# Attention and ternary feed-forward: transposes by halves of the tensor engine's rows, scores two steps behind the projection

## The reference

```python
# x = x + xattn(layernorm(x), ctx)
qh = einsum('bse,ehd->bshd', q, Wq)      # 16 heads of 32, in 4 groups
kh, vh = (einsum('bse,ehd->bshd', kv, W) for W in (Wk, Wv))   # 4 heads
qh, kh = rope(qh), rope(kh)
attn = softmax(einsum('bghsd,bhad->bhsa', qh, kh) / sqrt(32))  # sums over g
out = einsum('bhsa,bhad->bhsd', attn, vh).mean(axis=1) @ Wo
# x = x + ffn(layernorm(x)), weight ternary, input rounded to 8 bits by max|x|
out = einsum('bsk,ok->bso', clip(round(x / s), -128, 127), ternary(w)) * w_scale * s + bias
```

## Time and profile before

| | |
|---|---|
| Median of 3 runs | 1301.93 us |
| Profiled execution, its own time | 1300.03 us |
| Span of its instructions | 1298.1 us |
| Granted TensorE clock, mean | 0.993 |
| PE busy | 1265.4 us (97%), 9911 matmuls |
| Weight loads (PEld) | 1085.0 us (84%) |
| DVE busy | 1151.5 us (89%) |
| ACT busy | 1025.9 us (79%) |
| POOL busy | 792.1 us (61%) |
| Chain that ended last | PE 92%, DVE 4% |

### The profile page before, as it was taken

One profiled execution on the slowest core, in us unless ns is written; L12 is line 12 of the kernel. 1 busy time (PEld: TensorE's weight loads), 2 busy tenths in 40 slices (PEclk: granted clock), 3 DMA queues, 4 the chain that ended last, 5 costly groups with the idle time before them and its releaser, 6 DMA issues.

```text
span 1298.1 us, 36156 instructions
## 1 busy us (share of the span) xinstructions
PE 1265.4 (97%) x9911; PEld 1085.0 (84%) x9911; DVE 1151.5 (89%) x2577; ACT 1025.9 (79%) x2339; POOL 792.1 (61%) x1536
## 2 busy tenths in 40 slices
PE   7998999999999999999999999999969999999998
PEld 7898999999999999999999999999835555555554
DVE  4756999999999999999999999999978888888887
ACT  4565888888888888888888888888857888788876
POOL 4566888888888888888888888888810000000000
PEclk9999999999999999999999999999979999999999
DMA  9773455555555565546464633232109999999945
GB/s 297 225 207 105 140 177 166 170 171 167 175 161 181 152 189 151 190 144 196 143 197 141 197 116 103 75 105 73 37 32 362 405 397 397 405 396 405 398 202 223
DMA packets 101205, 265.26 MB, mean 204 GB/s; under 512 B 49833, under 2 KB 66153, under 8 KB 72498
## 3 DMA queue, kind: packets, MB, share of 16 engines
q1 hardware_dynamic: 101122, 264.79, 59.5%
q10 hardware_dynamic: 48, 0.07, 0.0%
HBM read 139.64 MB, written 125.17 MB: 204 GB/s over the span
## 4 chain that ended last, share of the span: by engine, by line
PE 92%; DVE 4%; issue 1%; POOL 1%; ACT 1%; DMA 0%; SPq 0%; POOLq 0%; DVEq 0%; ACTq 0%
PE bank L1156 17%; PE bank L1236 17%; PE bank L1204 13%; PE bank L1126 8%; PE bank L1191 8%; PE bank L1177 6%; PE bank L1227 4%; PE bank L1167 4%; PE bank L1234 4%; PE bank L1065 4%; PE bank L1138 2%; PE bank L1146 2%; PE bank L1054 1%; DVE amax L899 1%; DVE x_sb L929 0%
## 5 line engine op out<-in xcount | busy, mean ns | idle before, releaser
L1236 PE MATMUL bank<-wT,x_sb 128*128 128x512 f16 x1024 | 263.1, 379 | 0.0
L1156 PE MATMUL bank<-wqs,xT_sb 128*128 128x128 f32 x2048 | 259.7, 280 | 0.0
L731 ACT ACTIVATE x_sb<-bank,mean,cols 128x512 f32<-128x512 f32 x256 | 197.0, 775 | 66.6 <-PE bank L1236 66.5
L1156 PEld LDWEIGHTS bank<-wqs,xT_sb 128*128 128x128 f32 x2048 | 238.2, 191 | 6.6 <-ACT xT_sb L653 0.3
L1204 PE MATMUL bank<-v_blk,pT_sb 103*128 103x136 f32 x1536 | 199.0, 279 | 0.3 <-ACT pT_sb L695 0.3
L929 DVE SCALAR_TENSOR_TENSOR x_sb<-x_sb,mv_sb,bank 128x512 f32 (+1 forms) x256 | 179.9, 744 | 14.1 <-PE bank L1167 5.8
L1204 PEld LDWEIGHTS bank<-v_blk,pT_sb 103*128 103x128 f32 x1536 | 190.6, 190 | 0.5 <-ACT pT_sb L695 0.5
L1236 PEld LDWEIGHTS bank<-wT,x_sb 128*128 128x128 f16 x1024 | 100.4, 98 | 106.3 <-issue 0.8
L899 DVE TENSOR_REDUCE amax<-x_sb (+1 forms) x128 | 156.0, 1219 | 23.1 <-DVE bn_sb L890 10.1
L704 ACT ACTIVATE sq_sb<-x_sb 128x512 bf16 (+1 forms) x256 | 161.5, 631 | 18.7 <-DVE x_sb L929 1.4
L1004 DVE TENSOR_TENSOR x_sb<-x_sb 128x512 f32 (+1 forms) x256 | 164.7, 684 | 1.2 <-ACT x_sb L731 1.2
(11 more groups left out here) (132 smaller groups left out, 2558.2 us busy)
## 6 DMA issues: line engine op xcount, KB each, us to landing
out_y<-x_sb SPq DMA_DIRECT2D x112, 1024.0 KB, 7.2
x_sb<-in_x SPq DMA_DIRECT2D x64, 1024.0 KB, 6.4
x_sb<-out_y SPq DMA_DIRECT2D x48, 1024.0 KB, 8.9
x_sb<-in_ctx SPq DMA_DIRECT2D x38, 256.0 KB, 4.5
k_blk<-k_scr SPq DMA_DIRECT2D x256, 19.2 KB, 5.5
k_scr<-x_sb SPq DMA_DIRECT2D x38, 128.0 KB, 3.7
v_scr<-x_sb SPq DMA_DIRECT2D x38, 68.0 KB, 3.6
v_blk<-v_scr SPq DMA_DIRECT2D x128, 10.2 KB
```

What stands on the lines that cost most here:

```text
L731: act.activation(u_sb[:, t, :], bank[4 + t][:, :], ACT.Identity, bias=stat_of(mean1, j, t, back), scale=cols[:, 6:7]).then_inc(scaled_t, 1)
L1156: last = pe.matmul(bank[2][:, t * HD:(t + 1) * HD], xT_sb[:, t, c, :], wqs[:, c, :], start=c == 0, stop=c == EC - 1)
L1236: last = pe.matmul(bank[4 + t][:, :], q16T_sb[:, t, c, :], wT[:, c, :], start=False, stop=c == EC - 1)
```

## The change

In the main loop, every transpose of the tensor engine is written as two: rows 0 to 63 of the source and rows 64 to 127, into two neighbouring banks. The scores are plain float32, heads 0 and 1 on rows 0 to 63 and heads 2 and 3 on rows 64 to 127, into two banks; q and k are no longer split. PE's step begins with all transposes and the scores. A stage ROPE stands between PROJ and SCORE, so scores and all that follows are one step later. The orders of ACT, DVE and POOL within a step are changed. x is loaded by halves of a batch. On PE four of the waits take their value from registers. The keys' scratch and block have one part. Cut to its core:

```diff
-PROJ, SCORE, VALUE, HEAD, RESID, STAT, RSTD = range(7)
+HALF = P // 2
+PROJ, ROPE, SCORE, VALUE, HEAD, RESID, STAT, RSTD = range(8)
+xT_ps, qo_ps, sc_ps, pT_ps = (... psum_tensor(n, [P, 2, 512], F32) ...)
+bank = [ps[:, n, :] for ps in (xT_ps, qo_ps, sc_ps, pT_ps) for n in range(2)]
+def rows_of(ps, at0, n):
+    return ps[:, :, at0:at0 + n * HALF].rearrange("p h (c r) -> p c h r", c=n)
+def scores_of(t):
+    return sc_ps[:, :, t * SC // 2:(t + 1) * SC // 2].rearrange("p n (h a) -> p n h a", a=CTX)
 # SP
-sp.dma_start(x_sb[:, b, :, :], xv[b]).then_inc(x_in[b], 16)
+for n in range(2):      # in the loop each after at_least(sp, added_t, 4 * (b - XS) + 2 * n + 2)
+    sp.dma_start(x_sb[:, b, 2 * n:2 * n + 2, :], xv[b, :, 2 * n:2 * n + 2, :]).then_inc(x_in[2 * b + n], 16)
-                    batch_step(g * XS + k, k, g)
-                    kv_step(g * XS + k, k)
+                    batch_step(g * XS + k, k, g)
+                    v_fetch(g * XS + k - 1, k - 1)
+                    k_fetch(g * XS + k, k)
 # PE, one step
+def halves(ps, at0, src):
+    for n in range(2):
+        lo, hi = n * HALF, (n + 1) * HALF
+        last = pe.transpose(ps[0:src.shape[1], n, at0:at0 + HALF], src[lo:hi, :], ident[lo:hi, lo:hi])
+    return last
+if score or resid: at_least(pe, q_copied, i)
+if score:   # held: qr_ready
+    for t in range(2): last = halves(qo_ps, t * HALF, qr_sb[:, kj % 2, t * HD:(t + 1) * HD])
+if resid:   # held: ost_ready
+    for t in range(2): last = halves(qo_ps, P + t * HALF, ost_sb[:, t, ...])
+if proj:    # x_in, held: added_t >= 2 * (j - RESID)
+    for t in range(2):
+        for c in range(EC): last = halves(xT_ps, (t * EC + c) * HALF, x_sb[...])
+if value:   # pv_copied, held: exp_done_t
+    for t in range(2):
+        for c, start in enumerate(STARTS):
+            last = halves(pT_ps, (t * CHUNKS + c) * HALF, e_sb[:, kj % 2, t, start:start + CR])
+if score:   # k_in, sub_done_t >= 2 * j, qT_copied
+    for t in range(2):
+        for n in range(2):
+            lo, hi, w = n * HALF, (n + 1) * HALF, SC // 2
+            last = pe.matmul(sc_ps[:, n, t * w:(t + 1) * w], qT_sb[lo:hi, t * P:(t + 1) * P],
+                             k_blk[lo:hi, slot, n * w:(n + 1) * w], start=True, stop=True)
 # then, as before: projection (after oT_copied, xT_copied_t), y, values (after pT_copied_t)
 # ACT, one step:  pv, qT, oT, xT x2, pT x2, square(0), q, exponentials x2, square(1)
+act.activation(xT_sb[:, t, :, :].rearrange("p c (h r) -> p c h r", h=2),
+               rows_of(xT_ps, t * E // 2, EC), ACT.Copy).then_inc(xT_copied_t, 1)
 # DVE, one step:  reciprocal, variance (L876), amax, statistics 0, maxima x2, subtractions x2,
 #                 statistics 1, wait for them, residual adds x2, aggregates x2, wait, ve (L919)
-dve.tensor_tensor(qT_sb[:, 1, :], bank[3][:, 0:2 * P], qT_sb[:, 0, :].bitcast(F32), ALU.subtract)...
-    low_keys(j - 2)                       # setup: kT's low half, 39 times
 # POOL, one step: rope of pair i-1 (3), pw, pw2, rs, o, ost x2, mean, rs2
```

More of the change, by code:

```diff
@@ L518, in step @@
             def step(i, k, g):
[L519 to L525, removed]
+                proj, rope, score, value, head, resid, stat, rstd = (stage(i, k, g, lag) for lag in range(RSTD + 1))
+                if rope:
+                    j, kj, gj = rope
+                    at_least(pool, qr_ready, j)
+                    pool.wait_ge(q_copied, j + 1)
+                    half = slice(2 * (kj % 2), 2 * (kj % 2) + 2)
+                    for table, dst in ((qcos, qa_sb), (qsin, qb_sb)):
+                        pool.tensor_tensor(dst[:, :].rearrange("p (t h d) -> p t h d", t=2, h=HEADS),
+                                           q_sb[:, :].rearrange("p (t h d) -> p t h d", t=2, h=HEADS),
+                                           table[:, half, :].unsqueeze(2).broadcast_to([P, 2, HEADS, D]),
+                                           ALU.mult).then_inc(rope_mul, 1)
+                    at_least(pool, qT_done, j - 1)
+                    pool.wait_ge(rope_mul, 2 * j + 2)
+                    pool.tensor_tensor(qr_sb[:, kj % 2, :].rearrange("p (a b) -> p a b", b=2),
+                                       qa_sb[:, :].rearrange("p (a b) -> p a b", b=2),
+                                       swapped(qb_sb[:, :]), ALU.add).then_inc(qr_ready, 1)
                 if head:
@@ L560, in step @@
                                        ALU.add).then_inc(mean_ready, 1)
[L561 to L575, removed]
-                                       swapped(qb_sb[:, :]), ALU.add).then_inc(qr_ready, 1)
+                if rstd:
+                    j, kj, gj = rstd
+                    pool.wait_ge(var_ready, j + 1)
+                    pool.tensor_tensor(rs2[:, bass.ds(2 * j, 2)], ve2_sb[:, kj % 2, :], mhalf[:, :], ALU.pow)\
+                        .then_inc(rs2_ready, 1)
             steps(pool, step)
@@ L636, in step, with square @@
             def step(i, k, g):
-                proj, score, value, head, resid, stat, rstd = (stage(i, k, g, lag) for lag in range(RSTD + 1))
+                proj, rope, score, value, head, resid, stat, rstd = (stage(i, k, g, lag) for lag in range(RSTD + 1))
+                def square(t):
+                    j, kj, gj = stat
+                    act.wait_ge(added_t, 2 * j + t + 1)
+                    at_least(act, sq_done, 2 * j + t)
+                    act.activation(sq_sb[:, :], x1_at(kj, gj, t), ACT.Square,
+                                   accum_out=ssq[:, bass.ds(2 * j + t, 1)]).then_inc(sq_done, 1)
                 if head:
@@ L645, in step @@
                                    bank[6][:, 0:2 * HEADS * VC], ACT.Copy).then_inc(pv_copied, 1)
-                if proj:
-                    j, kj, gj = proj
-                    for t in range(2):
-                        act.wait_ge(xT_done_t, 2 * j + t + 1)
-                        if t == 0:
-                            at_least(act, q_done, j)
-                        act.activation(xT_sb[:, t, :, :].rearrange("p c r -> p (c r)"), bank[t][:, :],
-                                       ACT.Copy).then_inc(xT_copied_t, 1)
-                    if isinstance(j, int) and j == 0:
-                        keys_out(CT, CLAST)
                 if score:
@@ L1132, in step @@
+            def step(i, k, g):
+                proj, rope, score, value, head, resid, stat, rstd = (stage(i, k, g, lag) for lag in range(RSTD + 1))
+                if score or resid:
+                    at_least(pe, q_copied, min(i, NP_) if isinstance(i, int) else i)
                 if score:
                     j, kj, gj = score
-                    pe.wait_ge(qr_ready, j + 1)
+                    held(qr_ready, j + 1, qr_count, 1)
                     for t in range(2):
-                        last = pe.transpose(bank[3][:, t * P:(t + 1) * P], qa_sb[:, t * HD:(t + 1) * HD],
-                                            ident[:, :])
+                        last = halves(qo_ps, t * HALF, qr_sb[:, kj % 2, t * HD:(t + 1) * HD])
```

282 lines of the change are left out of this document (136 added, 146 removed).

## The result

| | before | after |
|---|---|---|
| Median | 1303.12 us (4 runs) | 1268.89 us (4 runs, 1268.15 to 1269.79) |
| Ratio to before, 95% interval | | 0.9739 (0.9722 to 0.9756) |
| Profiled execution | 1300.03 us | 1268.90 us |
| PE / DVE / ACT / POOL busy | 97 / 89 / 79 / 61% | 95 / 89 / 79 / 63% |

The change gains 2.6%. I had forecast 1263 us.

What follows compares the result with a forecast made beforehand. PE bounds the kernel at 6.552 us a pair; relieved to 5.98, it yields to DVE at 6.18, rounded to 6.20. 123 periods give -43.3, ends +4.1: 1260.8, plus 1.9 for the median, 1263 us; range 1236 to 1296.

Steps and rivals of the forecast that it cites:

- the forecast's own range: Whole kernel's time: 1250 to 1277 us around the forecast of 1263, given a chance of 0.54.
- Transposes by halves: PE's loop step: 18 tiles at 0.085 us each, 1.53 in place of 1.98 (bounds 1.08 and 2.16).
- the slower rival (b): PE's halves do not run side by side: 0.120 a tile, PE 7.14 us a pair, about 1379 us; chance 0.12.
- Scores: PE's loop step: plain f32 score matmuls on two overlapping halves, 0.52 us in place of 0.86.
- Changes of form: PE going from halves to the full array and back: 0.2 us a pair (bounds 0 and 0.4).
- DVE's step: DVE's loop step without the low-half subtraction of q takes over as bound: 6.18 us a pair, lower bound 5.79.
- The two waits: DVE's bare waits on its own results: 0.23 us at the residual adds, 0.16 at ve behind the aggregates.
- the period as one number: Main loop: 123 periods of 6.20 us in place of 6.552, giving -43.3 us.
- Ends: Fill and drain: pipeline eight deep in place of seven, one step more, +4.1 us (bounds 0 and 6.5); setup nothing.
- Signs of being wrong: In DVE's loop step, waits for PE or ACT over 0.2 us a pair, or L653, L695, L939 longer from two banks.

Runs made afterwards that it cites:

- half_by_half: The changed kernel, same matmuls reordered: in each group of transposes or scores, all pieces on rows 0 to 63, then all on 64 to 127; 1290.17 us.
- x_whole: The changed kernel with only the eight transposes of x, and ACT's reading of them, whole as before; 1305.36 us.
- before_x_halves: The kernel before the change, with only the eight transposes of x by halves and one signal for both row tiles; 1327.66 us, ratio 1.0197.
- dve_turn_of_16: The changed kernel with DVE's loop body written out for 16 steps, turning 7 times in place of 15; 1291.93 us.
- lag_one: The changed kernel with rope back in the projection's stage, seven stages, scores one step behind; 1385.74 us.
- the fastest kernel: The changed kernel with DVE's statistics wait behind the first residual add, ve moved ahead of the next step's amax, four exponentials' transposes of 128 columns; 1236.08 us.

## Why the prediction was right, and where its terms were off

The mechanism held. PE stopped being the bound, DVE's step took over, and nothing from ACT, POOL or the DMA queues came between. The number came out close partly by luck: the period was missed by 0.15 us, which is 17.6 us over 119 steps and alone would have given about 1280, past the 1277 of the forecast's own range, and ends that I had mis-sized took 9.5 of it back. Point by point:

- **Transposes by halves.** Taken at 0.085 a tile between 0.060 and 0.120; measured 0.065 for the twelve tiles of 128 columns and 0.092 for the six of 103, sum 1.33 for 1.53. The overlap itself, the question on which the slower rival (b) hung, is shown by half_by_half. The Trainium skill (TensorEngine Tiling, Key Properties) says that tiles load and multiply in parallel; the interleaved rows of half_by_half agree. The Trainium skill's rule for a weight load (TensorE: Matmul & The Clock Gate, Part 2, LDWEIGHTS), 107 ns for 128 columns, would not allow 0.065 us for two halves even if they load together, and not the 0.060 of a single one (0.06 in half_by_half as well); the measurement decides against it.
- **Scores.** 0.52 and a change of form at 0.1 were predicted, 0.70 is both together.
- **Changes of form.** 0.1 each was too low, 0.15 by x_whole and 0.14 by before_x_halves. All in all 5.98 predicted for PE, 5.86 measured free of waits.
- **DVE's step.** 6.18, rounded to 6.20; ordinary steps measure 6.23. The two waits were named and sized at 0.23 and 0.16. The first measures 0.24 to 0.36 as a gap; at the second, aggregates and ve take 0.64 (605.37 to 606.01) where I had 0.15 + 0.20 + 0.16. What I had not seen is what stands in them. The queue doesn't only wait for a signal there, it has addresses and counts to work out that it otherwise does while the engine runs.
- **The step that failed: the period as one number.** I multiplied 123 periods by 6.20 and left out the turn of the loop. Before, the turns cost next to nothing, since PE was ahead (6.59 against 6.55). With DVE as the bound and a wait for itself right ahead of the turn they cost 0.93 each, 13 us in all. dve_turn_of_16 shows it is DVE's.
- **Ends.** I added 4.1 us for the eighth stage. The end of the kernel did grow, by 3.2. But the first eight steps shrank by 7.5, where I had counted 1.4, since PE no longer waits for rope while the pipeline fills, and setup by 2.5, where I had said nothing. I can show the first in the timeline (steps of 3.4, 4.2 and 4.7 us for 5.2, 5.1 and 6.0). The second was not tested; the keys' subtractions and half of their stores are gone there.
- Together: -39.2 us was forecast from 1300.03 and -31.1 came. The turns are +13, the ordinary steps and the first, shorter turn +4.6, the ends -9.5 (6.1 in the first steps, 2.5 in the setup, 0.9 behind the loop).
- **Signs of being wrong.** They stayed out, but for a trace of one. DVE's waits for PE are 0.05 us a pair, and of the operations that now read two banks only ACT's copy of the exponentials is longer, 499 ns for 490.

That the x halves without the new order make the kernel slower (before_x_halves, with one signal for both row tiles), and the new order without the lag too (lag_one), I had not predicted, as I costed the parts as if each stood alone. The gain belongs to the three together. One part has no run of its own: that q is no longer split, which took the subtraction of 0.31 us (L913) out of DVE's step. With it DVE would need some 6.4 to 6.5 us (6.23 and 0.31, less what of ve's wait it would cover), and little would be gained; that is argued, not shown.

Open: what the 6.67 at a turn of the fastest kernel consists of, and what makes its residual adds late. Of the 0.33 us between its mean step of 6.08 and PE's own 5.75, 0.31 stand in front of the x transposes, which wait for the adds. Whether the ring through y or the one through the values, ACT's copy of them and DVE's reciprocal (46 waits, 11.6 us in 540) sets when the adds come, no run tells apart.

## What to carry to other kernels

Where two engines are within 5% of one another, cost the second one's step with its bare waits before believing in relief of the first: here DVE's waits for its own results also uncovered its queue's address work, and the branch of the loop, so put other work between producer and wait. Halves of the tensor engine's rows made small f32 transposes 1.7 times as fast here (0.110 to 0.065 us), but each change of form costs as much as three tiles save (0.15 against 0.045 each), so they must stand in one stretch, and the copy that the next matmul waits for needs other work beside it. Before writing out a longer loop body, look at its instruction transfers and at the granted clock behind each turn.

## What the runs showed of the hardware

- Two 64-row transposes on either half of the rows run together: 0.063 to 0.065 us a pair, where pieces on one half alone start 0.06 apart (half_by_half). A pair is four instructions, 0.016 each; the fastest rate seen before was 0.028.
- In such pairs 103 columns of stationary data take 0.091 us and 128 columns 0.063.
- A change between 64-row and 128-row matmuls costs 0.14 to 0.15 us, the mean of entering and leaving (x_whole, before_x_halves).
- A DVE loop body of eight steps turns for 0.93 us. With one of sixteen the step at the turn is 4 to 6.5 us longer: DVE stands 2.56 us, five instruction transfers of 8 KB come with each turn, and about 2.7 us are PE at the lower clock.
- After PE had stood 2.99 us its granted clock was 0.50 for 6.8 us (dve_turn_of_16); after 1.09 us it stayed 1.00 (changed kernel).
- Copies and maxima that read PSUM in two banks and runs of 64 or 154 columns take hardly longer or no longer: xT 595 ns in both kernels, the exponentials' copy 499 for 490, maxima 460 for 473.
